# Gate matmuls behind the weighted sums, and dense block 0's gates in memory of their own, in a cross-attention and mixture-of-experts kernel on one core

## What is computed

```python
def attention(q, k, v, Wq, bq, Wk, bk, Wv, bv, Wo, bo):
    Q, K, V = (project(...).reshape(bs, sl, 16, 32) for ...)
    weight = softmax(einsum('bshd,bsgd->bshg', Q, K), axis=-1)
    return einsum('bshg,bsgd->bshd', weight, V).reshape(bs, sl, 512) @ Wo.T + bo

x = x + attention(layernorm(x), ctx, ctx, ...)
z = layernorm(x)
topk_w, topk_idx = top_k(softmax(z @ gate_weight.T), 2)
y = routed experts of z, weighted by topk_w
y = y + (silu(z @ Wg.T) * (z @ Wu.T)) @ shared_down.T
x = x + y
```

## Time and profile before

| | |
|---|---|
| time, median of 3 runs | 1449.7 us (1448.55 to 1450.1) |
| the profiled execution's own time | 1446.31 us |
| its span | 1444.6 us |
| TensorE matmuls | 1340.1 us busy, 93% of the span |
| VectorE | 884.4 us, 61% |
| ScalarE | 674.4 us, 47% |
| GpSimd | 372.7 us, 26% |
| chain that ended last | TensorE 80%, VectorE 11%, issue 2%, ScalarE 2%, DMA 2% |

### The profile page before, as it was taken

How to read it: one execution, slowest core, us unless ns; L and a number is a source line. 1 busy time by engine, 2 the same in 40 slices (tenths; PEclk the granted TensorE clock), 3 DMA queues, 4 the chain that set the end, 5 groups by cost and what they waited for, 6 DMA issues and landing times.

```text
span 1444.6 us, 34230 instructions
## 1 busy us (share of the span) xinstructions
PE 1340.1 (93%) x11411; PEld 1005.0 (70%) x11412; DVE 884.4 (61%) x1952; ACT 674.4 (47%) x1500; POOL 372.7 (26%) x480
## 2 busy tenths in 40 slices
PE   4799999999999997788999999999999999999997
PEld 4688788888888885656767756666666666657675
DVE  6888888888888888667855532232232232224566
ACT  6276667777676776431444423333333333332121
POOL 4322222222222220004566011111111111104554
PEclk9899999999999998899999999999999999999999
DMA  5556766776767658497734622222222222227996
GB/s 197 134 141 190 198 196 185 204 204 199 189 185 202 185 138 270 129 350 134 113 53 83 148 95 81 80 86 80 81 85 82 80 86 81 81 72 235 315 312 225
DMA packets 212740, 223.20 MB, mean 155 GB/s; under 512 B 84693, under 2 KB 142109, under 8 KB 212334
## 3 DMA queue, kind: packets, MB, share of 16 engines
q1 hardware_dynamic: 193608, 178.62, 43.5%
q0 software_dynamic: 12880, 35.47, 8.1%
q10 hardware_dynamic: 6198, 8.40, 2.0%
HBM read 129.30 MB, written 67.96 MB: 137 GB/s over the span
## 4 chain that ended last, share of the span: by engine, by line
PE 80%; DVE 11%; issue 2%; ACT 2%; DMA 2%; SPq 1%; POOL 0%; DVEq 0%; POOLq 0%; ACTq 0%
PE psum_b L726 44%; PE psum_a L726 30%; PE psum_b L1016 2%; PE psum_b L1038 2%; DVE z_parts L1472 1%; DVE k_scale L1394 1%; DVE d_m L1705 1%; PE psum_b L752 1%; SPq L488 1%; DVE wdn L1791 1%; DMA heads<-in_wk_t 1%; DVE gate_act L1680 1%; ACT z_parts L1120 1%; DMA wgu_in<-base_rows 1%; PE psum_b L784 0%
## 5 line engine op out<-in xcount | busy, mean ns | idle before, releaser
L726 PE MATMUL psum_a<-wgu,zg_t 128*128 x1704 | 267.7, 314 | 2.1 <-DVE zg_t L1802 1.7
L726 PEld LDWEIGHTS psum_a<-wgu,zg_t 128*128 128x128 f16 x1704 | 166.1, 98 | 90.2 <-issue 10.3
L726 PE MATMUL psum_a<-zt_in,wsgu 128*128 128x256 f16 x1536 | 170.6, 273 | 1.0 <-ACT y_sb L1306 0.8
L2025 POOL DMA_INDIRECT zg<-z_rows,gather_ix x71 | 67.2, 946 | 402.9 <-DVE gather_ix L1798 395.8
L726 PEld LDWEIGHTS psum_a<-zt_in,wsgu 128*128 128x128 f16 x1536 | 148.8, 98 | 24.9 <-issue 6.5
L1807 DVE SCALAR_TENSOR_TENSOR silu<-psum_a,w_scale,silu 128x352 f32<-128x352 f32 x71 | 41.5, 584 | 191.1 <-ACT silu L1293 191.1
L726 PE MATMUL psum_b<-wdn,act_t 128*128 (+1 forms) x639 | 149.6, 379 | 1.6 <-DVE act_t L1814 1.6
L726 PE MATMUL psum_b<-wsdn,sh_t 128*128 128x512 f16 (+1 forms) x576 | 134.4, 388 | 14.9 <-DVE sh_t L1686 14.4
L1912 POOL TENSOR_SCALAR var_eps<-mv 128x1 f32<-128x1 f32 x64 | 28.4, 443 | 429.7 <-DVE mv L1371 289.9
L1293 ACT ACTIVATE silu<-psum_a,w_scale 128x352 f32<-128x352 f32 x71 | 39.4, 554 | 202.4 <-PE psum_a L726 202.4
L726 PEld LDWEIGHTS psum_b<-wsdn,sh_t 128*128 128x128 f16 (+1 forms) x576 | 54.6, 99 | 88.9 <-issue 18.3
(11 more groups left out here) (247 smaller groups left out, 2346.8 us busy)
## 6 DMA issues: line engine op xcount, KB each, us to landing
expert_rows<-y_sb SPq DMA_DIRECT2D x71, 256.0 KB, 2.0
k_st<-k_parts SPq DMA_DIRECT2D x192, 64.0 KB, 2.0
q_st<-q_parts SPq DMA_DIRECT2D x180, 64.0 KB, 2.0
wgu_in<-in_wgu_t SPq DMA_DIRECT2D x8, 1408.0 KB, 16.5
x_sb<-in_x SPq DMA_DIRECT2D x16, 512.0 KB, 5.5
cx_in<-in_ctx_t SPq DMA_DIRECT2D x16, 512.0 KB, 8.8
x_res<-in_x SPq DMA_DIRECT2D x16, 512.0 KB, 6.3
value_rows<-heads SPq DMA_DIRECT2D x16, 512.0 KB, 3.3
```

The source lines that it names most:

```text
L726: return nc.tensor.matmul(o, l, r, start=start, stop=stop)
L2025: pool.indirect_dma_start(out=zg[:, b, :], out_offset=None, in_=z_d[:, :], in_offset=bass.IndirectOffsetOnAxis(ap=gather_ix[:, b:b + 1], a ...
```

## The change

Two edits at once. *In the passes:* the gate matmuls go behind the weighted sums and write bank A0, the scores' own (step `R`; only behind the last pass does the step `L` in B2 stay); the turn of `c_rep` goes ahead of the turned logits, which also wait for the logits' copy; ScalarE makes both `z_t` before the first high half; VectorE has the context reduction and the copy into `c_rep` ahead of the low halves of z. *Around dense block 0:* its gates and hidden halves get a place in `wdn_in` that stage one doesn't use; ScalarE and VectorE interleave them with the rest of block 15; the Exp comes behind them; the eighth expert's load, which overwrites that place, waits for the end of block 0. In the last pass ScalarE's `weights_out` and `shared_high` alternate, and VectorE has the two scale searches behind the second pair of `shared_low`.

```diff
-ROUTE = [("L", "B2")]
+ROUTE = [("R", "A0")]
+LAST_ROUTE = [("L", "B2")]
...
-             + [("P0", "A2"), ("P1", "A3")] + TURN_ROUTE + BOUND)
+             + [("P0", "A2"), ("P1", "A3")] + BOUND + TURN_ROUTE)
...
+        gates_of_first = wdn_in[:, 2:4, :].rearrange("p e d -> p (e d)")[:, 0:GB * BT].rearrange("p (f t) -> p f t", f=GB)
+        hidden_of_first = wdn_in[:, 4:7, :].rearrange("p e d -> p (e d)").bitcast(F16).rearrange("p (h f t) -> p h f t", h=2, f=len(FS_CH))
...
             def load_expert(e):
+                if e == E - 1:
+                    sp.wait_ge(sh_out, SH_STEPS)
+                    settle(sp)
...
             def turn_logits(i):
                 wait_free(pe, "LT", i)
+                settle(pe)
+                wait_drained(pe, route_step(i), i)
                 settle(pe)
@@ TensorE, body
                     turn_z(i)
-                if behind:
-                    route(i)
                 attend(0, i)
                 attend(1, i)
                 if behind:
-                    turn_logits(i)
+                    route(i)
                 if ahead:
                     turn_bound(i)
+                if behind:
+                    turn_logits(i)
@@ ScalarE
             def z_out(i):
                 turned_out(i, 0)
+                turned_out(i, 1)
                 z_high(i, 0)
-                turned_out(i, 1)
...
                 if isinstance(i, int) and i == NB - 1:
+                    weights_out(0, i)
                     act.wait_ge(ws_loaded, 48)
                     act.wait_ge(ws_scaled, 1)
-                    shared_high(range(KC))
-                weights_out(0, i)
-                weights_out(1, i)
+                    shared_high(range(2))
+                    weights_out(1, i)
+                    shared_high(range(2, KC))
+                else:
+                    weights_out(0, i)
+                    weights_out(1, i)
...
+            attended_out(NB)
+            down_weights_high()
+            gate(0, 0)
+            gate(0, 1)
+            hidden_high(0, 0)
+            hidden_high(0, 1)
+            gate(0, 2)
+            gate(0, 3)
+            z_out(NB)
+            z_high(NB, 1)
+            hidden_high(0, 2)
+            hidden_high(0, 3)
+            gate(0, 4)
+            hidden_high(0, 4)
+            gate(0, 5)
+            hidden_high(0, 5)
+            act.wait_ge(r_shift, 1)
+            nc.scalar.activation(d_s[:, :, :], d_s[:, :, :], ACT.Exp).then_inc(r_exp, 1)
@@ VectorE, body
                 if isinstance(i, int) and i == NB - 1:
-                    find_scale(wsd_scale, psum_b[0][:, P:2 * P])
...
-                    find_scale(wd_scale, psum_b[0][:, 2 * P:3 * P])
-                    dve.sem_inc(wd_scaled, 1)
                     shared_low(0)
                     shared_low(1)
                 if ahead:
                     values_out(i)
+                if ahead2:
+                    weigh_context(i + 2)
+                if ahead:
+                    spread_context()
                 if behind:
                     z_low(i, 0)
                     logits_out(i)
                     z_low(i, 1)
-                if ahead2:
-                    weigh_context(i + 2)
-                if ahead:
-                    spread_context()
                 if weighs:
                     weigh_piece(i, weighs)
                 if isinstance(i, int) and i == NB - 1:
                     shared_low(2)
                     shared_low(3)
+                    find_scale(wsd_scale, psum_b[0][:, P:2 * P])
...
+                    find_scale(wd_scale, psum_b[0][:, 2 * P:3 * P])
+                    dve.sem_inc(wd_scaled, 1)
@@ VectorE, behind normalise_out(NB)
-            shared_block(0, 0, 0, nothing)
+            for f in range(2):
+                gate_times_up(0, f)
+            for f in range(2):
+                hidden_low(0, f)
+            z_low(NB, 0)
+            for f in range(2, 4):
+                gate_times_up(0, f)
+            logits_out(NB)
+            z_low(NB, 1)
+            for f in range(2, 4):
+                hidden_low(0, f)
+            turned_logits_out(NB)
+            for f in range(4, 6):
+                gate_times_up(0, f)
+                hidden_low(0, f)
+            wait_drained(dve, "LT", NB)
...
+            V.tensor_tensor(d_s[:, :, :], tok_scores[:, :, :], d_m[:, :].unsqueeze(2).broadcast_to([P, NT, E]), ALU.subtract).then_inc(r_shift, 1)
+            dve.wait_ge(base_loaded[0], 16)
+            add_shared(0, 0)
```

More of the change, by code:

```diff
@@ L86 @@
 IS_BEHIND = {name for name, _ in OUT + BEHIND + ROUTE + TURN_ROUTE}
+ONLY_LAST = {name for name, _ in LAST_ROUTE}
 def steps_of(i):
     names = [name for name, _ in FULL_PASS]
+    if i == NB:
+        return [n for n in names if n in IS_BEHIND - {"R"} | ONLY_LAST]
+    names = [name for name in names if name not in ONLY_LAST]
     if i < 0:
         return [n for n in names if n in IS_AHEAD]
-    if i == NB:
-        return [n for n in names if n in IS_BEHIND]
     return [n for n in names if not (i == 0 and n in IS_BEHIND) and not (i == NB - 1 and n in IS_AHEAD)]
@@ L105, in earlier_fills, with route_step @@
         return whole + sum(n in mine for n in names[:names.index(step)])
-    return (i - 1) * len(mine) + earlier_fills(step, 1)
+    return (i - 1) * len(mine - ONLY_LAST) + earlier_fills(step, 1)
+def route_step(i):
+    return "L" if isinstance(i, int) and i == NB else "R"
 class Chain:
@@ L923, in down @@
                 first = isinstance(i, int) and i == 0
+                hidden = gates_and_hidden(i)[1]
                 for fs in (range(n - 1), range(n - 1, n)):
@@ L934, in down @@
                             for hp, wp in PARTS:
-                                last = mm(sh_bank(n + s), sh_t[0:fn, hp, f, s * P:(s + 1) * P], wsdn[0:fn, wp, f, :],
+                                last = mm(sh_bank(n + s), hidden[0:fn, hp, f, s * P:(s + 1) * P], wsdn[0:fn, wp, f, :],
                                           f == 0 and (hp, wp) == PARTS[0], f == n - 1 and (hp, wp) == PARTS[-1])
@@ L1240, in hidden_high @@
                 act.wait_ge(sh_raw, i * len(FS_CH) + (f + 1))
-                copy(sh_t[0:fn, HI, f, :], gate_act[0:fn, f % GB, :]).then_inc(sh_high, 1)
+                gates, hidden = gates_and_hidden(i)
+                copy(hidden[0:fn, HI, f, :], gates[0:fn, f % GB, :]).then_inc(sh_high, 1)
             def gates(i, after):
@@ L1260, in weights_high16 @@
                                ACT.Copy, scale=w_scale[:, 2:3]).then_inc(w_high16, 1)
-            for f in range(len(FS_CH)):
-                gate(0, f)
-                if f > 0:
-                    hidden_high(0, f - 1)
-            hidden_high(0, len(FS_CH) - 1)
+            attended_out(NB)
[16 more added lines that the diff above has]
+            nc.scalar.activation(d_s[:, :, :], d_s[:, :, :], ACT.Exp).then_inc(r_exp, 1)
             gates(1, lambda f: None)
@@ L1575, in body @@
                 if isinstance(i, int) and i == NB - 1:
+                    shared_low(0)
+                    shared_low(1)
+                if ahead:
+                    values_out(i)
+                if ahead2:
+                    weigh_context(i + 2)
+                if ahead:
+                    spread_context()
+                if behind:
+                    z_low(i, 0)
+                    logits_out(i)
+                    z_low(i, 1)
+                if weighs:
+                    weigh_piece(i, weighs)
+                if isinstance(i, int) and i == NB - 1:
+                    shared_low(2)
+                    shared_low(3)
                     find_scale(wsd_scale, psum_b[0][:, P:2 * P])
@@ L1685, in hidden_low @@
                 dve.wait_ge(sh_high, i * len(FS_CH) + (f + 1))
-                V.tensor_tensor(sh_t[0:fn, LO, f, :], gate_act[0:fn, f % GB, :], sh_t[0:fn, HI, f, :], ALU.subtract).then_inc(sh_out, 1)
+                gates, hidden = gates_and_hidden(i)
+                V.tensor_tensor(hidden[0:fn, LO, f, :], gates[0:fn, f % GB, :], hidden[0:fn, HI, f, :], ALU.subtract).then_inc(sh_out, 1)
             def gated_hidden(i, after):
```

54 lines of the change are left out of this document (16 added, 38 removed).

## The result

The changed kernel is **slower**, by 1%: 1464.4 us (median of 8 runs, 1460.0 to 1471.0) against 1449.9 beside it, ratio 1.0101 with an interval of 1.0075 to 1.0127. The profiled execution took 1466.15 us, its span is 1464.4, against 1444.6 before: 19.8 us. The prediction had the sign, but 1455.4 and a top of 1460 were too low.

What follows compares the result with a forecast made beforehand. TensorE, busy 93% of the span, was taken as the bound, so its stops counted. Passes +2.6, pass 14 -0.1, last pass with block 0 0, block 2 +3.2: +5.7 us on the 1449.7 median, 1455.4 us, range 1441 to 1460.

Steps and rivals of the forecast that it cites:

- Step 1: Full passes: weighted sums start right behind the turns, at about 314.5, so the gate matmuls can go at 316.4.
- Step 2: Full passes: the c_rep copy arrives at 315.9, inside GpSimd's subtraction, and is held until that ends at 317.61.
- Rival A: Full passes: the c_rep copy isn't held, -0.9 us a pass, -11.7 in all; 1441.1 us, chance 0.14.
- Step 3: End of each full pass: next pass starts at 320.37, +0.2 us a pass, +2.6 us over 13 passes.
- The one visible price: Clock lost after a stop, read from block 0's down product after a 7.33 us stop: 9.76 - 8.04 = 1.7 us.
- Last pass: Pass 15: gate matmuls behind the sums and the scale searches delay block 0's gate_up by 7.0 us, plus 1.7 of clock.
- Block 0: Dense block 0: the 7.33 us stall shrinks to about 0.35 and the down product runs warm, -8.7 us.
- Block 2: Before dense block 2: late zt_in stops TensorE 5.5 us, plus 1.7 of clock, less 4.0 given back: +3.2 us.
- B: Last pass: v_p's landing is not what holds the sums; -0.3 us in all, 1449.4 us, chance 0.08.
- C: Block 2: zt_in lands in time as the loads drain faster; +2.5 us in all, 1452.2 us, chance 0.08.
- D: Block 0: its own memory changes nothing, another wait replaces the stall; +3.7 us more, 1459.1; chance 0.10 together with E.
- E: Blocks 4 to 6: later columns and base rows arrive too late, +3 us, 1458.4; chance 0.10 together with D.

Runs made afterwards that it cites:

- crep_reduced: The changed kernel in its own order, with c_rep written by a one-element VectorE reduction instead of a copy; 1448.8 us, ratio 1.0008 to the kernel before.
- low_first: crep_reduced with the low halves of Z0 and Z1 both ahead of the logits copy on VectorE; 1437.3 us, ratio 0.9893 to the kernel before.

## Why the prediction was wrong, point by point

- **Step 1** (sums no longer wait): right, and 322.80.
- **Step 2** (copy held to the end of the subtraction): right, 1.93 us, and crep_reduced shows the cause. Rival A didn't come.
- **Step 3, the step that failed.** It reckoned with +0.2 us a pass and put no clock into it. Its own term was a little too high: clean passes of after are 34.06 us apart, as before. In the clean pass that ends at 258.13, low Z1 ends at 256.40 + 0.68 = 257.08, so the next pass begins 1.05 us later where 1.14 was taken, and its first K product follows the turn of x after 0.84 us, in before after 1.13. But the stop it had itself worked out, 317.61 + 0.60 + 0.34 + 0.68 against sums and gate matmuls done by 317.1, was over 2 us in one piece, and the price of a stop was asked only in the last pass and block 2. "The one visible price" was not the only one: before's block 2 already ran at half clock among its waits of 1.49, 1.43 and 1.04 us (7.26 us for a down product that takes 5.46). Measured, 9 of 13 pass ends lose clock, 15.5 us in all, and the passes take +17.2 us instead of +2.5. These 14.7 us are the whole miss of the profiled execution: 19.8 is 14.1 more than the sum of 5.7, and the other terms cancel to -0.6. Between the medians, 9.0 us are missing (1464.4 against 1455.4).
- **Last pass:** +7.0 and +1.7 of clock; measured +6.1 to block 0, and 8.18 - 5.40 = 2.8 of clock. That the clock's price was 1.7 came from one row at another place and was too low. (The 2.3 taken for the searches is 2.46 by its own row, which changes nothing.)
- **Block 0:** -8.7 + 1.7 = -7.0; measured -6.0. The gains are as forecast (7.33 to 0.27 and 9.76 to 8.05, together -8.8), the difference being the first product's 2.8. ScalarE's two further table loads came and cost nothing:

```profile
614.90 1.28 ACT L1251 ACT_TABLE_LOAD   x1
...
640.63 1.28 ACT L1295 ACT_TABLE_LOAD   x1
...
642.44 1.28 ACT L1251 ACT_TABLE_LOAD   x1
```

- The sum "last pass and block 0 = 0" was right: +6.1 - 6.0, two misses of 1 us that cancel.
- **Block 2:** a stop of about 5.5 us, 1.7 of clock and 4.0 given back, +3.2; measured 5.08, and +5.2 - 3.1 = +2.1. That it came so near is partly luck: the clock cost 2.8 (13.48 - 10.65), only 3.1 of the 4.0 came back (one wait of 0.82 stays), and 2.4 of before's own clock loss came back, which the prediction hadn't seen.
- **Rivals:** B and C didn't come (6.06 us for v_p, 5.08 for zt_in). For D and E at most the 1.2 us of blocks 3 to 9 are left.

## What to carry to other kernels

When an order is changed on a full engine, add up where its idle time lands and not only how much it is: two stops of 1.54 and 0.45 us made into one of 2.32 left the clean passes' length as it was and cost 15.5 us of clock. Price each such stop at both levels of the clock, and look at the granted clock pass by pass. Beside a GpSimd instruction, ask which kind of VectorE instruction stands there: a one-line change of kind, and then a swap of two lines, turned a 1.0% loss into a 1.1% gain (low_first), and the mended last pass and the earlier `zt_in` made it 1.5 to 2.1%.

## What was not expected of the hardware

TensorE fell to half its clock after stops of 1.03 to 2.4 us in passes in which it is otherwise busy 31.7 of 34 us, and the same stop cost it at 10 pass ends or at 3, by 1.05 us of matmul less or more elsewhere in the pass. From one pass to the next the moment of the fall moved against the pass. Falls made a pass 1.2 to 2.3 us longer, several times the 0.2 us that had been weighed. Sixteen useless matmuls a pass made the kernel 8 us faster than after.
